# Attention on one core: row maxima run 12 steps ahead of the scores instead of 16, and the first tile's heads are divided in the attention's last step

## The chip, the cores and the metric

The kernel runs on one core of a Trainium2 chip. The metric is the device time of one execution in microseconds; the figure for a kernel is the median of several executions. A core has five engines that run side by side and wait for each other by semaphores: PE (matmul), DVE (vector), ACT (activation functions), POOL (general) and SP, which here issues all the transfers. Transfers run on 16 DMA engines.

## The reference

The program computes four residual layers on x of shape (4, 1024, 256): attention, a feed-forward layer with spikes, a selective scan, and the feed-forward layer again. Only the attention is touched.

```python
query = qt_c + qt_r            # 16 heads of 16, compact part plus rotary part
key = kt_c + kt_r
attn = jnp.einsum('bhqd,bhkd->bhqk', query, key) / scale
attn = jax.nn.softmax(attn, axis=-1)
out = jnp.einsum('bhqk,bhkd->bhqd', attn, value)
out = out.transpose(0, 2, 1, 3).reshape(b, s, d_model)
return out @ Wo_w + Wo_b
```

## The kernel before

**Stages.** `project` makes queries, keys and values of all eight tiles of 512 tokens and writes queries and keys, split in three bf16 parts each, to DRAM. `attend` works through 16 groups (4 batches x 4 groups of 4 heads). `merge_heads` divides the heads by the softmax sums, multiplies by Wo and adds to x, tile by tile. Each stage is a block: all engines leave it before the next one begins.

**A group in `attend`.** A group has 16 steps: 2 halves of the 512 queries by 8 tiles of 128 keys. In a step PE makes the scores of 4 heads in two pairs (L763), ACT takes exp of each pair (L826), and PE multiplies the probabilities of the step before by the values (`pv`, L809). Since exp needs the row maximum subtracted, three rows of the negated maxima (split in bf16 parts) stand below the queries in `qs`, and the keys have rows of ones. So all maxima of a half must be known before its first score. They come from scores made once more in the other orientation, 128 queries by 512 keys: 64 such units in a group, 4 in each step, PE's `for_max` (L749) into three banks in turn, DVE's `maximum` (L840).

**How far ahead.** In the 16 steps of group g all 64 units of group g + 1 are made, so the maxima run 16 steps ahead. Those of group 0 are made at the end of `project`: 32 pairs of units, each one reduction of 128x1024 (L499). The last group makes none.

**From maxima to rows.** When a half's 32 units are there, DVE merges the two key halves (`both_halves`, L846), PE transposes (`turn`, L756), DVE negates (L853), POOL splits in four instructions (`split`, L703 to L711), and SP sends three rows into `qs` (`max_rows`, L632). The transposition is done in step `TURN_NOW` = 2 for half 1 of this group and in step `TURN_NEXT` = 10 for half 0 of the next. PE waits for the rows of half 0 ahead of step 0 and for those of half 1 ahead of step 8 (`max_rows_in`).

**Order on the queues.** All orders are written out by hand. SP per group: rows of half 1, the 13 loads of queries and keys of group g + 2 (`load_stack`), rows of half 0 of g + 1, the stores of both halves of the output (`o_to_dram`, L636). POOL: split of half 1, values of g + 1 (`v_of`), split of half 0 of g + 1, bias addition. Loop: PE, DVE, ACT and POOL go through 5 turns of 3 groups, and the last group stands by itself after it.

**The last group** also prepares the division of batches 0 to 2 (`early_batches`): SP loads the softmax sums and the heads of tiles 0 to 2 (L540), DVE takes reciprocals and splits them (`split_recips`, L547 to L555) in step 4, SP writes the parts to DRAM (L650), waits, and reads them back in another layout (`recip_heads`, L654). `merge_heads` does the same for batch 3 and then loads the heads of tiles 3 to 7 when their buffers are free. For each tile PE spreads the reciprocals over the heads' rows (`spread_tile`, L1022), DVE multiplies (`divide`, L1068), PE projects (L1032) and DVE adds (L1075).

## Time and profile before

| | us |
|---|---|
| median of 3 runs | 2026.62 |
| lowest, highest | 2025.83, 2028.26 |
| profiled execution | 2029.69 |
| its span | 2027.7 |

Stages in the span: projection up to 183.8 (its last 38 us are the maxima of group 0), attention 184.4 to 937.3, merge 939.8 to 978.3, then feed-forward, scan and feed-forward up to the end. Busy over the span: PE 92%, DVE 80%, ACT 54%, POOL 34%; the mean granted clock of PE is 0.957 of full speed.

A line of a time line gives start, duration, engine, source line, operation, tiles (output <- input, partitions x elements, type) and how many instructions are drawn together; in brackets the idle time of the engine before it and who ended it. SPq stands for SP's transfer issues; their duration is that of issuing, not of landing.

### The profile page before, as it was taken

What the parts mean: (1) busy time and instruction counts of PE and PEld (TensorE: products, weight loads), DVE (VectorE), ACT (ScalarE), POOL (GpSimd) and SP (SyncE); (2) the same over time, 40 slices, a digit from 0 to 9 for tenths busy, and PEclk for the clock granted to TensorE, in tenths of its full rate; (3) what the DMA queues carried; (4) which work ended last, traced back from release to release, by engine and by line L of the source; (5) the groups of instructions that cost most, each with busy time, mean ns of one, the idle gap of its engine ahead of it and who ended that gap; (6) DMA issues with size and microseconds to landing.
All of it is one profiled execution on the core that took longest, in us unless ns stands there. A gap on an engine that the chain in (4) does not pass through costs nothing. (4 is left out here: it accounts for less than half of the span.)

```text
span 2027.7 us, 25794 instructions
## 1 busy us (share of the span) xinstructions
PE 1868.1 (92%) x7414; PEld 826.8 (41%) x7414; DVE 1625.9 (80%) x2596; ACT 1087.7 (54%) x1511; POOL 697.9 (34%) x474
## 2 busy tenths in 40 slices
PE   7898999999999999999999997798889877789998
PEld 4441332332322322323676663333333333356665
DVE  6878998998998988974556666999999999955654
ACT  5552665666665666674244335766576657333321
POOL 3561000001100000010000015999999999800000
PEclk9996998999998999999999997899999999899999
DMA  4850222122221122203210003455545545400000
GB/s 134 175 129 13 62 51 42 45 43 44 46 45 44 43 48 38 48 12 122 82 42 21 22 23 118 126 143 136 135 121 142 137 122 164 99 6 16 22 21 21
DMA packets 100394, 147.13 MB, mean 73 GB/s; under 512 B 15089, under 2 KB 54401, under 8 KB 98721
## 3 DMA queue, kind: packets, MB, share of 16 engines
q1 hardware_dynamic: 100256, 145.42, 28.6%
q8 instruction: 72, 1.18, 0.3%
q14 instruction: 66, 0.53, 0.1%
HBM read 114.69 MB, written 30.29 MB: 71 GB/s over the span
## 5 line engine op out<-in xcount | busy, mean ns | idle before, releaser
L840 DVE TENSOR_REDUCE mx<-max_bank 128x1 f32<-128x512 f32 x960 | 618.1, 687 | 65.0 <-PE max_bank L749 64.7
L826 ACT ACTIVATE probs<-score_bank 128x1024 f32<-128x1024 f32 x512 | 496.9, 1021 | 289.7 <-PE score_bank L763 288.8
L749 PE MATMUL max_bank<-ks,qs 96*128 96x512 bf16 x960 | 336.0, 390 | 0.0
L763 PE MATMUL score_bank<-qs,ks 99*128 99x512 bf16 x1024 | 313.6, 388 | 14.5 <-issue 10.4
L1639 PE MATMUL ys_bank<-outs,rec_diag 128*128 128x512 f32 x512 | 260.2, 642 | 67.3 <-POOL outs L1582 43.5
L1574 POOL TENSOR_TENSOR ring<-u,bc 128x1024 f32<-128x1024 f32 x128 | 300.6, 2359 | 0.4 <-DMA bc<-bc_scr 0.3
L809 PE MATMUL o_bank<-probs,vg 128*32 128x512 f32 x2048 | 275.5, 610 | 0.5 <-ACT probs L826 0.5
L1780 ACT ACTIVATE a_bank<-dt,decay_s 128x512 f32<-128x512 f32 x256 | 170.7, 686 | 150.5 <-DVE ring L1904 98.1
L1582 POOL TENSOR_TENSOR outs<-ring,bc 128x1024 f32<-128x1024 f32 x102 | 239.9, 2352 | 13.6 <-DVE ring L1904 13.6
L1252 PE MATMUL y_bank_f<-wpr_f,hid_f 128*128 128x256 f32 x1024 | 236.4, 379 | 0.0
L703 POOL CAST neg_parts<-neg_max 16x128 bf16<-16x128 f32 x31 | 8.7, 282 | 639.1 <-DVE neg_max L853 639.1
L1252 PEld LDWEIGHTS y_bank_f<-wpr_f,hid_f 128*128 128x128 f32 x1024 | 193.4, 190 | 59.9 <-issue 38.3
L1324 ACT ACTIVATE relu_f<-hid_bank_f 128x512 f32<-128x512 f32 x128 | 76.3, 596 | 250.9 <-PE hid_bank_f L1243 225.3
L749 PEld LDWEIGHTS max_bank<-ks,qs 96*128 96x128 bf16 x960 | 94.1, 98 | 281.1 <-DVE mx L840 187.1
L1895 DVE SCALAR_TENSOR_TENSOR ring<-a_bank,ring 128x512 f32<-128x512 f32 x256 | 172.6, 674 | 22.5 <-ACT a_bank L1780 21.6
L1639 PEld LDWEIGHTS ys_bank<-outs,rec_diag 128*128 128x128 f32 x512 | 99.3, 202 | 207.6 <-issue 114.9
L1414 DVE SCALAR_TENSOR_TENSOR hid_f<-hid_bank_f,relu_f 128x512 f32<-128x512 f32 x128 | 86.9, 688 | 97.0 <-ACT relu_f L1324 95.2
L763 PEld LDWEIGHTS score_bank<-qs,ks 99*128 99x128 bf16 x1024 | 99.6, 100 | 123.1 <-issue 27.4
L1904 DVE TENSOR_TENSOR_SCAN ring<-a_bank,state,ring 128x512 f32<-128x512 f32 x100 | 127.8, 1278 | 0.0
L1904 DVE TENSOR_TENSOR_SCAN ring<-a_bank,ring 128x512 f32<-128x512 f32 x104 | 126.3, 1214 | 0.0
L1243 PE MATMUL hid_bank_f<-xn_f,wfc_f 128*128 128x512 f32 x256 | 116.5, 592 | 1.1 <-PEq L972 1.1
L1613 PE MATMUL work<-xn_s,wtap_s 128*128 128x512 f32 x224 | 107.0, 616 | 7.3 <-DVE x L1876 7.3
(233 smaller groups left out, 1933.7 us busy)
## 6 DMA issues: line engine op xcount, KB each, us to landing
bc<-bc_scr SPq DMA_DIRECT2D x128, 512.0 KB, 5.0
qk_parts<-parts SPq DMA_DIRECT2D x128, 96.0 KB, 1.9
qs<-qk_parts SPq DMA_DIRECT2D x128, 64.0 KB, 4.3
o_scr<-o_sb SPq DMA_DIRECT2D x32, 256.0 KB, 2.0
ks<-qk_parts SPq DMA_DIRECT2D x16, 384.0 KB, 4.7
xn_s<-xn_scr SPq DMA_DIRECT2D x8, 515.0 KB, 6.3
x<-in_x_dram SPq DMA_DIRECT2D x8, 512.0 KB, 4.3
ks<-qk_parts SPq DMA_DIRECT2D x16, 256.0 KB, 3.5
```

The costliest lines, as they stand in the source:

```text
L749: nc.tensor.matmul(max_bank[(r + a) % MB][:], qs[r][0:SROWS, half, j, qt * P:(qt + 1) * P], ks[r][0:SROWS, j, kh * TW:(kh + 1) * TW], star ...
L763: mm = nc.tensor.matmul(score_bank[pair][:, j % 2], ks[r][0:MROWS, j, kt * P:(kt + 1) * P], qs[r][0:MROWS, qh, j, :], start=True, stop=True)
L809: mm = nc.tensor.matmul(o_bank[32 * j:32 * j + 32, :], vg[r][:, kt, j], probs[:, s % 2, j], start=(kt == 0), stop=(kt == QT - 1))
L826: nc.scalar.activation(probs[:, s % 2, 2 * pair:2 * pair + 2], score_bank[pair][:], ACT.Exp, scale=SOFTMAX_SCALE).then_inc(probs_ready, 1)
L840: nc.vector.tensor_reduce(mx[:, a // HU, a % HU:a % HU + 1], max_bank[(r + a) % MB][:], AX_X, ALU.max)\
L1252: mm = nc.tensor.matmul(y_of(b), hid[:, f, b * P:(b + 1) * P], wpr[:, f], start=(f == 0), stop=(f == FC - 1))
L1574: nc.gpsimd.tensor_tensor(ring[:, g % RING], u[t % 2][:], bc[:, g % BC, 0:1].to_broadcast([P, DC, TW]), ALU.mult).then_inc(inputs, 1)
L1582: nc.gpsimd.tensor_tensor(outs[:, g % OUTS], ring[:, g % RING], bc[:, g % BC, 1:2].to_broadcast([P, DC, TW]), ALU.mult).then_inc(weighted, 1)
L1639: mm = nc.tensor.matmul(y_bank[f][:], rec_diag[:, f * NS + n], outs[:, g % OUTS, f], start=(n == 0), stop=(n == NS - 1))
L1780: nc.scalar.activation(a_bank[g % 2][:, f], dt[:, t % 2, f], ACT.Exp, scale=a_col[:, f, n:n + 1])\
L1895: nc.vector.scalar_tensor_tensor(x, a, 1.0, x, ALU.subtract, ALU.mult).then_inc(scaled, 1)
L1904: nc.vector.tensor_tensor_scan(a if on_dve(g) else x, a, x, state[:, f, n:n + 1] if t % TPB else 0.0, ALU.mult, ALU.add)\
```

## The change

`AHEAD_STEPS` = 12 sets how far the maxima run ahead, and `STILL` = 4 follows from it.

- In the projection 24 pairs are made instead of 32. The pairs of half 1 (n from 16) keep the maxima of the two key halves apart, in `mx`, so that group 0 can finish them.
- In steps 0 to 3 of each group the last 16 units of that same group are made, in steps 4 to 15 the first 48 of the next (`maxima_of`). The last group thus makes 16 units too.
- The key halves are merged at the end of steps 3 and 11, and `TURN_NOW`, `TURN_NEXT` become 4 and 12. PE waits for the next group's queries and keys in step 4 instead of step 0.
- PE no longer waits for the first memset of the values' tile at the start.
- In the last group DVE's `split_recips` is done in step 9 instead of step 4. Ahead of the last product PE waits for the read-back reciprocals and spreads those of tile 0; DVE waits for the loaded heads and divides tile 0, ahead of its last copy (`divide_tile`). `merge_heads` starts with tile 1.
- SP's wait for the stored outputs moves from the end of `attend` into `merge_heads`, behind the load of `ident` and ahead of that of the sums. DVE's `split_recips` there comes behind the division of tile 1.

```diff
+AHEAD_STEPS = 12
+
+
 def first_groups(m):
...
         ("qs0", [P, 2, G, TW], BF16), ("qs1", [P, 2, G, TW], BF16), ("ks0", [P, G, S], BF16), ("ks1", [P, G, S], BF16),
-        ("ident", [P, P], F32), ("row_max", [P, 2, units // 2], F32), ("neg_max", [units // 2, 2, P], F32),
+        ("ident", [P, P], F32), ("mx", [P, 2, units], F32), ("row_max", [P, 2, units // 2], F32), ("neg_max", [units // 2, 2, P], F32),
         ("neg_rest", [units // 2, 2, P], F32), ("neg_parts", [units // 2, 2, 3, P], BF16), ("b_row", [P, D], F32))}
...
         PAIRS = G * QT
+        FIRST_PAIRS = 2 * AHEAD_STEPS
         max_banks = (rot_banks, comp_banks)
...
             pe.wait_ge(stack_in, 2 * STACK_LOAD)
-            for n in range(PAIRS):
+            for n in range(FIRST_PAIRS):
                 half, j, qt = n // (PAIRS // 2), n % (PAIRS // 2) // 4, n % 4
...
             nc.vector.tensor_tensor(begun["b_row"][:], bias_bank[:, 0:D], bo[:], ALU.add).then_inc(bias_kept, 1)
-            for n in range(PAIRS):
+            for n in range(FIRST_PAIRS):
                 half, i = n // (PAIRS // 2), n % (PAIRS // 2)
                 dve.wait_ge(unit_ready, n + 1)
-                nc.vector.tensor_reduce(row_max[:, half, i:i + 1], max_banks[n % 2][:].rearrange("p a t -> p (a t)"),
-                                        AX_X, ALU.max).then_inc(unit_max, 1)
+                if half == 0:
+                    nc.vector.tensor_reduce(row_max[:, 0, i:i + 1], max_banks[n % 2][:].rearrange("p a t -> p (a t)"),
+                                            AX_X, ALU.max).then_inc(unit_max, 1)
+                else:
+                    nc.vector.tensor_reduce(begun["mx"][:, 1, 2 * i:2 * i + 2], max_banks[n % 2][:], AX_X, ALU.max)\
+                        .then_inc(unit_max, 1)
                 if n == PAIRS // 2 - 1:
...
                         .then_inc(neg_ready, 1)
-            dve.wait_ge(unit_max, PAIRS)
+            dve.wait_ge(unit_max, FIRST_PAIRS)
...
-    return {n: m.sb(n, shape, dt, side="right") for n, shape, dt in (
+    early = {n: m.sb(n, shape, dt, side="right") for n, shape, dt in (
         ("recip_heads", [3 * H, B, S], BF16), ("o_in", [P, LOADED, DC, TW], F32), ("wo", [P, DC, D], F32),
-        ("head_rows", [3 * H, D], F32), ("head_parts", [3 * H, D], BF16))}
+        ("head_rows", [3 * H, D], F32), ("head_parts", [3 * H, D], BF16), ("o_sb", [P, 2, TW], F32),
+        ("o_n", [P, 2, DC, TW], F32))}
+    early["o_out"] = [m.sem(f"o_out{i}") for i in range(2)]
+    early["spread"], early["divided"] = m.sem("spread"), m.sem("divided")
+    return early
+
+
+def divide_tile(nc, dve, t, o_n, o_in, bank, spread, divided):
+
+    for c in range(DC):
+        dve.wait_ge(spread, DC * t + c + 1)
+        nc.vector.tensor_tensor(o_n[:, t % 2, c], o_in[:, t % LOADED, c], bank[c][:], ALU.mult).then_inc(divided, 1)
...
     MB = 3
-    TURN_NOW, TURN_NEXT = 2, 10
+    STILL = STEPS - AHEAD_STEPS
+    TURN_NOW, TURN_NEXT = STILL, STILL + QT
     with ExitStack() as ctx:
...
         probs = m.sb("probs", [P, 2, G, TW])
-        mx = m.sb("mx", [P, 2, HU])
+        mx = begun["mx"]
         ident, row_max, neg_max, neg_rest, neg_parts = (
             begun[n] for n in ("ident", "row_max", "neg_max", "neg_rest", "neg_parts"))
-        o_sb = m.sb("o_sb", [P, 2, TW])
+        o_sb, o_n = early["o_sb"], early["o_n"]
         EARLY = (B - 1) * H
...
         o_kept = m.sem("o_kept")
-        o_out = [m.sem(f"o_out{i}") for i in range(2)]
+        o_out, spread, divided = (early[n] for n in ("o_out", "spread", "divided"))
         sums_in, recip_split, recips_out, recips_in, early_in = (
...
-            return max_bank[(r + 1 + 4 * (s + 1)) % MB]
+            return max_bank[(r + 4 * (s + 1 + AHEAD_STEPS)) % MB]
+
+        def maxima_of(g, r, s, i):
+
+
+            if s < STILL:
+                return g, r, 4 * (s + AHEAD_STEPS) + i
+            return g + 1, (r + 1) % 3, 4 * (s - STILL) + i
...
                 body(g, g % 3, g < NGT - 1, g < NGT - 2)
-            for h in range(2):
-                sp.wait_ge(o_out[h], 16 * NGT + 16)
             sp.wait_ge(recips_in, 48)
...
             pe.sem_inc(pv_done, 3 * STEPS)
-            pe.sem_inc(max_ready, UNITS)
+            pe.sem_inc(max_ready, 4 * AHEAD_STEPS)
             pe.sem_inc(turned, 1)
...
                         pe.wait_ge(ones_set, 4)
-                    if s == 0 and with_next:
+                    if s == STILL and with_next:
                         pe.wait_ge(stack_in[(r + 1) % 3], it * STACK_LOAD + STACK_LOAD * (1 + (r + 1) // 3))
...
                         scores(g, r, s, pair)
-                        if with_next:
+                        if with_next or s < STILL:
                             if s in (TURN_NOW + 1, TURN_NEXT + 1) and pair == 0:
...
                                 pe.wait_ge(neg_ready, g * 2 + (2 if s == TURN_NOW + 1 else 3))
-                            for_max(g + 1, (r + 1) % 3, 4 * s + pair)
-                    if with_next:
-                        for_max(g + 1, (r + 1) % 3, 4 * s + 2)
+                            for_max(*maxima_of(g, r, s, pair))
+                    if with_next or s < STILL:
+                        for_max(*maxima_of(g, r, s, 2))
                     if s > 0:
...
-                            pe.wait_ge(reduced, g * UNITS + UNITS + 4 * s + 2 + MB)
+                            pe.wait_ge(reduced, g * UNITS + 4 * (s + AHEAD_STEPS) + 2 + MB)
                         turn(g if s == TURN_NOW else g + 1, 1 if s == TURN_NOW else 0, turn_bank(r, s))
-                    if with_next:
-                        for_max(g + 1, (r + 1) % 3, 4 * s + 3)
+                    if with_next or s < STILL:
+                        for_max(*maxima_of(g, r, s, 3))
+                if not with_next:
+                    pe.wait_ge(head_set, 1)
+                    pe.wait_ge(recips_in, 48)
+                    pe.wait_ge(neg_ready, g * 2 + 2)
+                    for c in range(DC):
+                        nc.tensor.matmul(max_bank[c][:], head_parts[:, c * P:(c + 1) * P], recip_heads[:, 0, 0:TW],
+                                         start=True, stop=True).then_inc(spread, 1)
                 if r == 2 or not with_next:
...
-            pe.wait_ge(ones_set, 1)
             groups(pe, body)
...
         def _(dve):
-            dve.sem_inc(reduced, MB + UNITS)
-            dve.sem_inc(row_max_ready, 2)
+            dve.sem_inc(reduced, MB + 4 * AHEAD_STEPS)
+            dve.sem_inc(row_max_ready, 1)
             dve.sem_inc(neg_ready, 1)
...
                             keep_o(g, 0)
-                        if with_next:
-                            maximum(g + 1, (r + 1) % 3, 4 * s + i)
-                        elif s == 4 and i == 0:
+                        if with_next or s < STILL:
+                            maximum(*maxima_of(g, r, s, i))
+                        elif s == QT + 1 and i == 0:
                             dve.wait_ge(sums_in, 16)
                             split_recips(nc, dve, sums, recip_parts, recip_split)
-                    if s == QT - 1 and with_next:
+                    if s == STILL - 1:
+                        both_halves(g, 1)
+                    if s == STILL + QT - 1 and with_next:
                         both_halves(g + 1, 0)
-                if with_next:
-                    both_halves(g + 1, 1)
+                if not with_next:
+                    dve.wait_ge(early_in, 16 * DC * LOADED)
+                    divide_tile(nc, dve, 0, o_n, o_in, max_bank, spread, divided)
                 if r == 2 or not with_next:
...
         PT = 8
-        recip_heads, o_in, wo, head_parts = (early[n] for n in ("recip_heads", "o_in", "wo", "head_parts"))
+        recip_heads, o_in, wo, head_parts, o_n, o_out, spread, divided = (
+            early[n] for n in ("recip_heads", "o_in", "wo", "head_parts", "o_n", "o_out", "spread", "divided"))
         sums = m.sb("sums", [H * PT, S // PT])
         recip_parts = m.sb("recip_parts", [H * PT, 3, S // PT], BF16)
-        o_n = m.sb("o_n", [P, 2, DC, TW])
         spread_bank = [m.bank(f"spread_bank{c}") for c in range(DC)]
...
         heads_in = [m.sem(f"heads_in{i}") for i in range(LOADED)]
-        spread, divided, out_ready, x_new = (m.sem(n) for n in ("spread", "divided", "out_ready", "mh_x_new"))
+        out_ready, x_new = m.sem("out_ready"), m.sem("mh_x_new")
         by_rows = o_scr.rearrange("g (j r) t -> (g j) r t", r=2 * HD)
...
+            sp.dma_start(ident[:], io["ident"]).then_inc(ident_in, 16)
+            for h in range(2):
+                sp.wait_ge(o_out[h], 16 * B * NG + 16)
             sp.dma_start(sums[:], by_rows[HEADS0:, HD, :].rearrange("g (h t) -> g h t", h=PT)).then_inc(sums_in, 16)
-            sp.dma_start(ident[:], io["ident"]).then_inc(ident_in, 16)
             sp.wait_ge(recip_split, 5)
...
-            spread_tile(0)
             for t in range(NT):
...
                     dve.wait_ge(out_ready, DC * (t - 1))
-                for c in range(DC):
-                    dve.wait_ge(spread, DC * t + c + 1)
-                    nc.vector.tensor_tensor(o_n[:, t % 2, c], o_in[:, t % LOADED, c], spread_bank[c][:], ALU.mult)\
-                        .then_inc(divided, 1)
+                divide_tile(nc, dve, t, o_n, o_in, spread_bank, spread, divided)
...
-            divide(0)
-            dve.wait_ge(sums_in, 16)
-            split_recips(nc, dve, sums, recip_parts, recip_split)
             for t in range(NT):
...
                     divide(t + 1)
+                if t == 0:
+                    dve.wait_ge(sums_in, 16)
+                    split_recips(nc, dve, sums, recip_parts, recip_split)
                 if t == 3:
...
```

## Rows read from the trace of the kernel before

**Rows 1.** Table of stretches, core 0, 193 to 238.5 us: busy us of each engine, clock, DMA.
```profile
193.00:238.50 45.50, 45.50 (x262) 13.80 (x258) 42.12 (x69) 30.82 (x32) 4.58 (x10) 1.00 0.22 48
```

**Rows 2.** Time line of DVE, the projection's tail: start us, us, what.
```profile
173.20 1.22 DVE L499 TENSOR_REDUCE row_max<-comp_banks 128x1 f32<-128x1024 f32 x1
...
182.61 1.22 DVE L499 TENSOR_REDUCE row_max<-comp_banks 128x1 f32<-128x1024 f32 x1
```

**Rows 3.** Time line of SP's queue, the same tail.
```profile
171.50 1.86 SPq L239 DMA_DIRECT2D qs<-neg_parts  x3
```

**Rows 4.** DMA issues, 165 to 176 us: issue xcount, KB each, us to landing.
```profile
qs<-neg_parts SPq DMA_DIRECT2D x3, 4.0 KB, 1.7
```

**Rows 5.** Time line, the first group's start: POOL and PE.
```profile
184.41 0.53 POOL L686 MEMSET vg<- 128x512 f32 x1 [12.93 <-POOLq L139]
...
185.46 1.03 PE L763 MATMUL score_bank<-qs,ks 99*128 99x512 bf16 x2 [2.90 <-POOL vg L686]
```

**Rows 6.** Time line of PE, first group: the first scores of two steps.
```profile
199.03 0.60 PE L763 MATMUL score_bank<-qs,ks 99*128 99x512 bf16 x2
...
201.86 0.60 PE L763 MATMUL score_bank<-qs,ks 99*128 99x512 bf16 x2
```

**Rows 7.** Time line of PE: transpositions either side of one turn of the loop.
```profile
310.34 0.28 PE L756 MATMUL max_bank<-ident,row_max 128*16 128x128 f32 x1
...
340.62 0.28 PE L756 MATMUL max_bank<-ident,row_max 128*16 128x128 f32 x1
```

**Rows 8.** Time line of the last group, all engines.
```profile
900.90 0.19 DVE L846 TENSOR_REDUCE row_max<-mx 128x16 f32<-128x32 f32 x1
901.07 1.04 PE L763 MATMUL score_bank<-qs,ks 99*128 99x512 bf16 x4
...
905.30 1.04 PE L763 MATMUL score_bank<-qs,ks 99*128 99x512 bf16 x4
...
909.53 1.14 PE L763 MATMUL score_bank<-qs,ks 99*128 99x512 bf16 x4
...
909.80 1.77 SPq L632 DMA_DIRECT2D qs<-neg_parts  x3
...
920.19 0.69 DVE L859 COPY o_sb<-o_bank 128x512 f32<-128x512 f32 x1
...
920.27 0.34 SPq L650 DMA_DIRECT2D recip_scr<-early_parts  x1
...
935.44 1.06 PE L809 MATMUL o_bank<-probs,vg 128*32 128x512 f32 x8 [0.47 <-ACT probs L826]
...
936.57 0.69 DVE L859 COPY o_sb<-o_bank 128x512 f32<-128x512 f32 x1 [15.69 <-PE o_bank L809]
```

**Rows 9.** DMA issues, 900 to 950 us: issue xcount, KB each, us to landing.
```profile
recip_scr<-early_parts SPq DMA_DIRECT2D x1, 288.0 KB, 6.6
recip_heads<-recip_scr SPq DMA_DIRECT2D x3, 96.0 KB, 2.9
```

**Rows 10.** Time line of the merge, all engines.
```profile
939.78 0.59 SPq L995 DMA_DIRECT2D sums<-o_scr  x1
...
942.74 5.43 PE L1032 MATMUL out_bank<-wo,o_n 128*128 128x256 f32 x16
...
947.34 1.26 SPq L540 DMA_DIRECT2D o_in<-o_scr  x2
...
952.29 0.60 PE L1022 MATMUL spread_bank<-recip_heads,head_parts 48*128 48x512 bf16 x2
...
953.74 1.29 DVE L1068 TENSOR_TENSOR o_n<-o_in,spread_bank 128x512 f32<-128x512 f32 x2 [0.65 <-DMA o_in<-o_scr]
...
956.48 0.60 PE L1022 MATMUL spread_bank<-recip_heads,head_parts 48*128 48x512 bf16 x2
```

**Rows 11.** Table of stretches, core 0: an idle of PE and what followed.
```profile
1652.40:1656.10 3.70, 0.00 (x0) 0.00 (x0) 3.70 (x6) 1.85 (x4) 3.70 (x3) 1.00 0.46 123
1656.10:1659.50 3.40, 3.35 (x4) 1.14 (x4) 3.40 (x5) 0.14 (x1) 3.40 (x2) 0.52 0.32 108
```

## The prediction

> **What bounds the kernel now.** The profiled execution took 2029.69 us, its span 2027.7; the median of the three runs is 2026.62. I work out a difference in the profiled execution and take it from all three, since the change adds no work that depends on the run. The change touches four stretches, so I read each with the view that shows its pace.
>
> First the table of stretches: in the loop over groups PE is busy in all of its 45.50 us at full clock, DVE in 42.12 and ACT in 30.82 [rows 1]. A step with maxima is 201.86 - 199.03 = 2.83 us long, PE-bound [rows 6]. Second the time line of the projection's tail: one reduction of a pair follows the other on DVE without a gap; nothing else is left to do there [rows 2]. Third the last group, which makes no maxima: its steps 2 and 3 take 909.53 - 905.30 = 4.23 us, 2.115 each, set by ACT, for whose exponentials PE waits, and steps 0 to 3 together 909.53 - 901.07 = 8.46 [rows 8]. Last, the start of the merge: a wait for stored outputs, a new block, a chain of small transfers, and only then a steady PE [rows 10].
>
> **Part 1, eight pairs leave the projection.** Pair 24 (counted from 1) starts at 173.20, pair 32 at 182.61: eight pairs are 9.41 us, all of it on DVE and on the path [rows 2]. The reduction of 128x1024 into two columns instead of one reads the same elements; I cost that at nothing, and at most 8 x 0.05 us if the second output column mattered. What is late next is the other thing that the projection's end waits for: the three rows of negated maxima of half 0. SP issues them from 171.50 for 1.86 us [rows 3], each lands 1.7 us after its issue [rows 4]; the last was issued about 172.7, so it lands at 174.4. DVE's new last reduction ends at 173.20 + 1.22 = 174.42. They tie. I take **-9.3**, between -9.4 and -8.7 (the landing is read from a median).
>
> **Part 2, PE no longer waits for the first memset.** Its first score came at 185.46 with POOL's memset named, while POOL itself began at 184.41 and needed 0.53 [rows 5]. PE could have started at most about 1.0 earlier, and at least 0 if its own entry takes as long. I take **-0.5**. The value tile is still waited for, a step and a half later.
>
> **Part 3, sixteen units move into the last group.** Counts per group are otherwise equal: 64 units in every one, now 16 of this group and 48 of the next. Steps 0 to 3 of the last group go from 8.46 to 4 x 2.835 = 11.34 us: **+2.9**. PE's time in which it waited for ACT is already subtracted in this. The range is 2.7 to 3.2, for DVE's copy of the other half's output falls among the four steps.
>
> **Part 4, the rows of maxima have four steps, not six.** From the start of the step that transposes, the chain transposition, negation, four POOL instructions and three SP issues was 909.80 + 1.77 - 905.30 = 6.3 us [rows 8]; the last of three issues begins 0.6 before the end of 1.77, and with 1.7 to land [rows 4] it is 7.4. In a group with maxima it has 4 x 2.84 = 11.3 us; in the last group 4 x 2.115 = 8.46. Both cover it, the second by 1.1 only. SP's 13 stack loads follow the rows of half 1 in the queue as before and end well before the rows of half 0, eight steps later, as before. POOL's copies of values and the bias additions keep their places behind the splits. Scores of the next half are queued behind such a wait on PE, and ACT and DVE behind them; cost **0**, at most 0.5 in the last group. The merging of both key halves (0.19 us on DVE [rows 8]) now comes one step ahead of the transposition; DVE has (45.50 - 42.12) / 16 = 0.21 us idle per step to take it [rows 1], so 0, between -0.1 and +0.1 for each of 31.
>
> **Part 5, the early denominators come later, and the last step waits for them.** Let T be the start of step 4 of the last group. Before, everything counted from step 2 (905.30). SP's rows go out at T + 4.5 to T + 6.3, then the sums, then six loads of heads, as before [rows 8]. DVE's five instructions now start behind its copy of the first half: that ran at 920.19, 10.66 after step 4, for 0.69. So they run from T + 11.4 to T + 17.1 (before, they ended at 920.24). The write of the parts was issued at 920.27 and landed 6.6 us later, at 926.9, which is 21.6 after 905.30, because the loads of heads and weights stood before it; the readback took 0.85 to its last issue and 2.9 to land [rows 9]. The loads drain at the same T + 21 now. If the write lands with them, at T + 21.6, the readback lands at T + 25.4. PE is through with the product of step 14 at 935.44 - 0.47 = 934.97 = T + 25.4. So the new wait is almost exactly covered. Behind it stand the two spreading matmuls (0.60 us [rows 10]) and the last product, which before started at 935.44 (T + 25.9) after ACT [rows 8]; it starts at T + 26.1 to 26.5. DVE divides for 1.29 before its last copy [rows 10], which starts at about T + 27.5 where it started at 936.57 = T + 27.0 [rows 8]: **+0.5**. Bounds: +0.2 when the readback is early, +2.3 when the write takes its whole 6.6 us from T + 17.1.
>
> The write of 288 KB shows 6.6 us behind the loads [rows 9]. The Trainium skill, "DMA: Bandwidth & Descriptors", section "Queues, rings and completion order", says that each DMA engine takes descriptors in ring order; by it the new, later write still leaves with the loads and ends at T + 21.6, where a transfer that overtook them would end at about T + 20. The first gives the +0.5, the second +0.35.
>
> **Part 6, the merge.** Let K be the end of the last copy, 937.26 before. The next block began at 939.78 = K + 2.5, behind the landing of the stored outputs; without that wait it begins at about K + 0.7, for the block of the attention began at 184.41, 0.58 after DVE's last reduction had ended at 183.83 [rows 2, 5]. Tile 0 is divided already, so its projection can start at K + 1.5 instead of K + 5.5. That would be 4 us, but the load of tile 3 stands in the way. It is issued behind sums, split, write and readback of the last batch: 947.34, and DVE already waited 0.65 us for it, until 953.74 = K + 16.5 [rows 10]. That chain starts from the landing of the stored outputs, which doesn't move; it wins only the block's entry, of which I take 0.4 us (the whole was 0.58). So DVE has tile 3 divided at K + 16.1 + 1.3 = K + 17.4, and PE, which before started spreading tile 4 at 956.48 = K + 19.2, starts then: -1.8. From there PE's pace holds, 956.48 - 952.29 = 4.19 us per tile [rows 10]. But PE would have ended tile 2 at about K + 13.6: it stands idle for 3.8 us where it was busy. An idle of 3.70 us at full clock was followed by 3.40 us at 0.52, that is the 1.2 GHz level [rows 11]. Half of 3.4 is 1.7 us lost. The sum is **-0.1**, between -1.8 (the clock holds, or PE is slow from the block's start and so has no idle) and +1.7 (the low level lasts 7 us).
>
> **Sum:** -9.3 - 0.5 + 2.9 + 0 + 0.5 - 0.1 = -6.5 us. Span 2021.2, profiled execution 2023.2, median **2020.1**.
>
> One thing varies by itself: where the loop turns over (after every third group) PE stops and the clock falls. Eight steps are 22.7 us; across the first such point it was 340.62 - 310.34 = 30.28, 7.6 more [rows 7]. There are four of them; I allow 3 us either way for all.
>
> **The rivals.**
> (a) The clock holds in the merge, part 6 gives -1.8: 2018.4. For it: PE is low from the start if the block's entry idles it long enough. Against it: [rows 11]. Chance 0.2.
> (b) Tile 3's load isn't the gate, since it lands sooner in an emptier queue; the merge then gives 4.0 and, if the clock holds too, 1.8 of its first projection (5.43 where a later one has 4.19 - 0.60): -12.2, 2014.4. Against it: DVE already waited for it. 0.08.
> (c) The readback is late (+2.3, not +0.5) and the clock low for long in the merge (+1.7, not -0.1): -2.9, 2023.7. 0.13.
> (d) Slower: the rows of maxima are late in every half of a group. Place: PE's wait ahead of the first score of a half. The price is what the chain lasts beyond four steps, about 31 times; it decides from 11.3 us, where the chain shows 7.4. Another POOL or SP item ahead of it worth 4.7 us would make 0.8 x 31 = 25, less the 6.5: 2045. Such an item, the stack loads, stands behind it in the queue. 0.04.
> (e) The change doesn't do what it says: the projection's end isn't DVE's but a transfer's, so eight pairs free nothing; 2029.4. [rows 2] to [rows 4] speak against it. 0.02.
>
> **How the numbers follow.** The forecast has 0.53, with its own range of 2017.5 to 2022.5. Its parts' bounds, the clock at the loop's turns and cases (a) and (c) give 2014.5 to 2024.5; left out are (d), (e), and (b), which lies at the lower end. What a measurement here can tell from no change is 0.2%, 4.05 us. Within it lie (c), (e) and 0.03 of the forecast's: 0.18. Slower is (d), 0.04, and faster the rest, 0.78.
>
> **What would show it.** The projection's last reduction at 174.4 and POOL's memset 9.3 earlier than 184.41; PE's first score about 0.5 behind it or less. Steps of 2.84 through step 3 of the last group. No idle of PE ahead of scores of a half. In the last step PE idle under 0.5 us for the readback. In the merge a PE idle of 3 to 4 us ahead of the spreading of tile 4, ended by DVE, which waited for the load, and a granted clock of 0.5 behind it. Wrong would be: rows of maxima that PE waits for, an idle over 1 us ahead of the last product, or PE steady from the first tile.

## The result, and the profile after

| | before | after |
|---|---|---|
| median, us | 2027.44 (4 executions) | 2016.18 (4 executions) |
| lowest to highest | 2025.83 to 2028.5 | 2011.42 to 2018.74 |
| profiled execution / its span | 2029.69 / 2027.7 | 2018.74 / 2016.9 |
| ratio | | 0.9936, 95% interval 0.9924 to 0.9948 |

The change is faster, by 11.3 us between the medians (13 by the ratio) where -6.5 was forecast. With the executions of the later studies, in which both kernels were run again unchanged, the means are 2028.1 (113 executions, standard error 0.25) and 2017.24 (17, standard error 0.9): **-10.9 us**, 95% interval about -12.7 to -9.1. That is the number to be explained.

The page of the changed kernel, its head and first row: PE is as busy as before (92%).

```profile
span 2016.9 us, 25815 instructions
PE 1862.0 (92%) x7414; PEld 828.5 (41%) x7414; DVE 1627.6 (81%) x2605; ACT 1087.4 (54%) x1511; POOL 697.9 (35%) x474
```

The time line of the changed kernel where projection turns into attention, as [rows 2, 3, 5] for before:

```profile
169.61 1.86 SPq L243 DMA_DIRECT2D qs<-neg_parts  x3
...
171.31 1.22 DVE L507 TENSOR_REDUCE mx<-comp_banks 128x2 f32<-128x1024 f32 x1
173.14 0.53 POOL L711 MEMSET vg<- 128x512 f32 x1 [3.55 <-POOLq L142]
...
174.08 1.03 PE L788 MATMUL score_bank<-qs,ks 99*128 99x512 bf16 x2 [2.82 <-SPq L647]
```

The first pair began at 144.04 in this execution and at 145.94 in that of before, so starts are compared as distances from it. The last reduction ends at 172.53, 28.49 behind the first pair: pair 24 of before ended at 28.48. A reduction of 1.22 us is as long as it was. PE's first score comes 1.55 us behind the last reduction; before, it came 1.63 behind.

The last group on PE, as [rows 8]:

```profile
884.54 1.06 PE L841 MATMUL o_bank<-probs,vg 128*32 128x512 f32 x8
885.54 0.60 PE L788 MATMUL score_bank<-qs,ks 99*128 99x512 bf16 x2
...
889.32 1.07 PE L841 MATMUL o_bank<-probs,vg 128*32 128x512 f32 x8
890.32 0.39 PE L774 MATMUL max_bank<-ks,qs 96*128 96x512 bf16 x1
890.54 0.60 PE L788 MATMUL score_bank<-qs,ks 99*128 99x512 bf16 x2
...
896.21 1.03 PE L788 MATMUL score_bank<-qs,ks 99*128 99x512 bf16 x4
897.17 1.06 PE L841 MATMUL o_bank<-probs,vg 128*32 128x512 f32 x8
898.17 0.28 PE L781 MATMUL max_bank<-ident,row_max 128*16 128x128 f32 x1
```

Steps 0 to 3 run from 885.54 to 896.21: 10.67 us. Steps 2 and 3 last 2.84 each (890.54 to 896.21); 0 and 1 together 5.00, since the product that belongs to step 0 was already done ahead of it (884.54) and only one follows until 890.54. With T = 896.21, the rest of that group on SP, DVE and PE:

```profile
900.70 1.77 SPq L659 DMA_DIRECT2D qs<-neg_parts  x3
...
913.20 0.34 SPq L677 DMA_DIRECT2D recip_scr<-early_parts  x1
917.87 1.26 SPq L681 DMA_DIRECT2D recip_heads<-recip_scr  x3
```

```profile
907.48 3.34 DVE L566 RECIPROCAL early_sums<-early_sums 96x512 f32<-96x512 f32 x1
...
912.49 0.69 DVE L574 TENSOR_TENSOR early_parts<-early_sums,early_parts 96x512 bf16<-96x512 f32 x1
922.38 1.29 DVE L552 TENSOR_TENSOR o_n<-o_in,max_bank 128x512 f32<-128x512 f32 x2 [9.20 <-PE max_bank L826]
923.58 0.68 DVE L890 COPY o_sb<-o_bank 128x512 f32<-128x512 f32 x1
```

```profile
921.90 0.59 PE L826 MATMUL max_bank<-recip_heads,head_parts 48*128 48x512 bf16 x2 [0.25 <-issue]
922.42 1.06 PE L841 MATMUL o_bank<-probs,vg 128*32 128x512 f32 x8
```

The rows of maxima go out at T + 4.49, the readback at T + 21.66, the spreading is at T + 25.69 with an idle of 0.25 before it, the last copy begins at T + 27.37. With K = 924.26, the end of that copy, the merge shows on PE and in the table of stretches (us, PE busy, granted clock, DMA share, GB/s):

```profile
925.23 0.59 PE L1058 MATMUL spread_bank<-recip_heads,head_parts 48*128 48x512 bf16 x2 [1.75 <-PEq L591]
925.75 3.72 PE L1068 MATMUL out_bank<-wo,o_n 128*128 128x256 f32 x16
...
934.12 3.72 PE L1068 MATMUL out_bank<-wo,o_n 128*128 128x256 f32 x16
940.83 1.03 PE L1058 MATMUL spread_bank<-recip_heads,head_parts 48*128 48x512 bf16 x2 [2.99 <-DVE o_n L552]
941.79 6.58 PE L1068 MATMUL out_bank<-wo,o_n 128*128 128x256 f32 x16
```

```profile
937.84:940.83 2.99, 0.00 (x1) 0.99 0.48 145
940.83:944.30 3.47, 3.47 (x8) 0.50 0.54 201
944.30:960.00 15.70, 15.70 (x62) 0.89 0.67 208
```

PE idles 2.99 us ahead of the spreading for tile 4 and is then granted half its clock, for the 3.47 us of the second row and longer: a mean of 0.89 over the 15.7 us of the third row is about 3.4 us more, so 6.8 us in all. The spreading takes 1.03 us instead of 0.60 and the sixteen matmuls behind it 6.58 instead of 3.72, together 3.3 us lost. On DVE it is the load of tile 3 that ends the wait:

```profile
939.49 1.28 DVE L552 TENSOR_TENSOR o_n<-o_in,spread_bank 128x512 f32<-128x512 f32 x2 [5.10 <-DMA o_in<-o_scr]
```

**Stretch by stretch.** Each number is a mean of five profiles. Before: the kernel before three times and two with one wait moved or left out, which changed nothing (before_again, before_third, before_late_wait, before_no_memset_wait, all below). After: the changed kernel four times and one with a wait moved, which changed nothing either (after_again, after_third, after_fourth, after_wait0).

| stretch | before | after | difference | forecast |
|---|---|---|---|---|
| first pair of maxima to first score | 39.50 | 30.06 | -9.44 | -9.8 |
| first score to first transposition | 10.47 | 15.47 | +5.00 | |
| first to last transposition, without the loop's turns | 594.67 | 595.23 | +0.56 | |
| last transposition to last product | 28.18 | 24.02 | -4.16 | |
| last product to end of last copy (K) | 1.82 | 1.85 | +0.03 | |
| these four together | 635.14 | 636.57 | +1.43 | +3.4 |
| four turns of the loop, 8 steps each | 115.64 | 113.98 | -1.66 | 0 |
| K to the feed-forward's first matmul | 41.67 | 41.49 | -0.18 | -0.1 |
| sum | | | -9.85 | -6.5 |

The rows for the transposition move by two steps with it (from step 2 to step 4), so only their sum means something. Ahead of the first pair and behind the merge nothing is changed: the first pair begins anywhere from 141.7 to 146.6 us in these ten profiles, and the stretch behind the merge scatters by 5 us, in kernels of either kind. The merge's own difference has a standard error of 0.4 us, that of the first group 0.4, that of the turns 1.2.

### The profile page after: what moved, and what is told of

Same layout as the page of the kernel before. It is cut to its first block and busy times, and to the rows that moved or that the text cites. A ratio compares the mean times of both kernels' runs of the same rounds, so it can differ in the third digit from the quotient of the medians.

```text
span 2016.9 us, 25815 instructions
## 1 busy us (share of the span) xinstructions
PE 1862.0 (92%) x7414; PEld 828.5 (41%) x7414; DVE 1627.6 (81%) x2605; ACT 1087.4 (54%) x1511; POOL 697.9 (35%) x474
## 5 line engine op out<-in xcount | busy, mean ns | idle before, releaser
L871 DVE TENSOR_REDUCE mx<-max_bank 128x1 f32<-128x512 f32 x976 | 628.1, 687 | 62.4 <-PE max_bank L774 61.3
L1927 DVE SCALAR_TENSOR_TENSOR ring<-a_bank,ring 128x512 f32<-128x512 f32 x256 | 171.5, 670 | 22.5 <-ACT a_bank L1812 21.6
```

What stands on the lines that cost most here:

```text
L871: nc.vector.tensor_reduce(mx[:, a // HU, a % HU:a % HU + 1], max_bank[(r + a) % MB][:], AX_X, ALU.max)\
L1927: nc.vector.scalar_tensor_tensor(x, a, 1.0, x, ALU.subtract, ALU.mult).then_inc(scaled, 1)
```

## The experiments

### Which part of the change brings it

Four kernels ran together: both kernels again, and each half of the change by itself. maxima_only is the changed kernel with tile 0 divided in `merge_heads`, as before (SP's wait for the stored outputs and DVE's `split_recips` of the last batch go back to their old places with it):

```diff
-                if not with_next:
-                    dve.wait_ge(early_in, 16 * DC * LOADED)
-                    divide_tile(nc, dve, 0, o_n, o_in, max_bank, spread, divided)
...
+            spread_tile(0)
...
+            divide(0)
```

merge_only is the changed kernel with the maxima 16 steps ahead, all reductions and PE's wait for the memset as before, and the split of the early denominators in step 4, as before:

```diff
-AHEAD_STEPS = 12
+AHEAD_STEPS = 16
...
-    TURN_NOW, TURN_NEXT = STILL, STILL + QT
+    TURN_NOW, TURN_NEXT = 2, 10
...
-                elif s == QT + 1 and i == 0:
+                elif s == 4 and i == 0:
```

> The kernel before, unchanged, for a second profile. Theory 1 (the part of the gain that the forecast lacks is the chance of PE's clock, at the four turns of the loop and ahead of the projection's tail): ratio 1.000, but the transpositions either side of the four turns, 116.8 us in all in the first profile, are 2 us or more off that here, and so is the first reduction of a pair, at 145.9 in the first. Theory 2 (the change itself shortens these stretches): both within 1 us of the first profile.

> The changed kernel, unchanged, for a second profile and a surer ratio. The first profile has 113.3 us across the four turns and the first pair at 144.0. Theory 1: these scatter here by 2 us or more as well, and the ratio lies nearer to the 0.9955 that the local differences of the stages touched make (-9.5 tail, -0.5 first group, +2.2 and +0.3 last group, +0.6 merge: -6.9, plus the start of the first group). Theory 2: 113.3 and 144.0 come again, within 1 us, and the ratio is 0.994 or lower.

> Only the maxima: 12 steps ahead, 24 pairs in the projection, no wait for the first memset, early reciprocals in step 9. Tile 0 is divided in the merge as before. Theory 1: -9.5 - 0.5 + 2.2 = -7.8 us, ratio 0.996. Theory 2 with the hidden gain on this side: -11 to -13 us, ratio 0.994.

> Only the merge: maxima 16 steps ahead as before, early reciprocals in step 4, but tile 0 divided in the last step, and SP's wait for the stored outputs in the merge. Theory 1: the last copy 0.3 us later and the merge 0.6 longer for its idle and low clock, +0.9 us, ratio 1.0005. Theory 2 with the hidden gain on this side: -3 us or more, ratio 0.9985 or lower.

| kernel | median, us | ratio to before |
|---|---|---|
| before_again | 2027.55 (12 executions) | 1.0003 (0.9990 to 1.0016) |
| after_again | 2018.05 (6) | 0.9940 (0.9921 to 0.9960) |
| maxima_only | 2014.49 (6) | 0.9938 (0.9915 to 0.9962) |
| merge_only | 2028.28 (12) | 1.0000 (0.9990 to 1.0010) |

The whole effect is that of the maxima. Dividing tile 0 early is worth nothing (parts 5 and 6 together, forecast +0.4). In merge_only the spreading in the last step falls into the time in which PE waited for ACT and costs nothing: the last product starts 28.18 us behind the last transposition, as before, the last copy ends level, and the merge behind it took 42.85 us.

The expectations set two theories against each other, chance at the turns and a gain that the change brings. The two profiles did not decide: after_again's turns took 116.6 us where the first profile had 113.3, and its first pair began at 146.6 instead of 144.0, as chance would have it; its ratio stayed at 0.9940, as the other theory would.

### The turns of the loop

Across the first turn before took 7.6 us more than eight steps inside the loop [rows 7]. The table of stretches (PE alone) of before at this turn, the pause and what follows:

```profile
324.69:328.60 3.91, 1.39 (x13) 0.98 0.19 73
328.60:338.23 9.63, 9.63 (x26) 0.50 0.02 4
338.23:340.62 2.39, 2.39 (x14) 0.91 0.00 0
```

The same in maxima_only, whose first turn stayed at full clock after a pause as long:

```profile
314.14:316.55 2.41, 0.00 (x1) 1.00 0.27 103
316.55:326.20 9.65, 9.65 (x51) 1.00 0.02 7
```

In 9.6 us the first got through 26 matmuls and the second 51. I first thought of the one wait that stands in step 0 in the kernel before and in step 4 in the changed one, that of PE for the next group's queries and keys. Two kernels move it alone: after_wait0 (the changed kernel, the wait back in step 0) and before_late_wait (the kernel before, the wait behind the first pair of scores).

```diff
-                    if s == STILL and with_next:
+                    if s == 0 and with_next:
```

```diff
                     for pair in range(2):
                         scores(g, r, s, pair)
+                        if s == 0 and with_next and pair == 0:
+                            pe.wait_ge(stack_in[(r + 1) % 3], it * STACK_LOAD + STACK_LOAD * (1 + (r + 1) // 3))
```

Two more, before_flat and after_flat, write the loop over groups of either kernel out straight on all engines, so that there are no turns:

```diff
-            with eng.Fori(0, (NGT - 1) // 3) as it:
+            for it in range((NGT - 1) // 3):
```

> The kernel before with the attention's loop over 15 groups written out straight, on all engines, so that nothing turns over. Three profiles of kernels with 16 steps ahead have 116.0 us across the four turns where 4 x 22.9 = 91.6 would be the pace inside; so -24 us, ratio 0.988. If the pause at a turn is the fetch of instructions and comes in straight code too, nothing.

> The changed kernel, written out straight in the same way. Theory A (what the forecast lacks lies in the turns: the changed kernel loses less to PE's low clock behind them): it differs from before_flat by the sum of the local differences alone, -9.5 tail - 0.2 first group - 0.2 pace + 2.5 last group + 0.4 merge = -7.0 us, so -31 against the kernel before, ratio 0.985. Theory B (the missing gain lies elsewhere): it stays 11 to 12 us under before_flat, ratio 0.982 or 0.983.

> The changed kernel with one piece undone: PE waits for the next group's queries and keys in step 0, as before, not in step 4. Theory A1 (this wait with its register arithmetic stands ahead of the first score behind each turn and lengthens PE's pause): pause 2.66 us on average instead of 2.54, low clock 7.6 us instead of 5.1 per turn, 4 us longer than the changed kernel, ratio 0.996. Theory A2 (chance, or another piece): as the changed kernel, 0.994.

> The kernel before with that same wait behind the first pair of scores of step 0 instead of ahead of it. Theory A1: the pause at a turn is 0.1 us shorter and the low clock behind it rarer, -4 us, ratio 0.998. Theory A2: 1.000.

| kernel | median, us | ratio to before |
|---|---|---|
| before_flat | 2008.28 (5) | 0.9895 (0.9879 to 0.9910) |
| after_flat | 1999.81 (4) | 0.9866 (0.9849 to 0.9882) |
| after_wait0 | 2017.05 (7) | 0.9951 (0.9934 to 0.9968) |
| before_late_wait | 2027.71 (12) | 0.9998 (0.9990 to 1.0007) |

The wait is not it: put back, it leaves the changed kernel where it was, and put later, it leaves before where it was. Written straight, the kernel before is 20 us faster, where 24 were expected. The four turn stretches alone fall by 22.8 us (115.6 to 92.9) and the other groups by 2.1, but in the seven straight profiles the first pair of maxima begins 3.8 us later than in the 13 with a loop (147.9 and 144.1 in the mean); why is not shown. In before_flat the same place (PE alone) has no pause and full clock throughout:

```profile
324.00:345.00 21.00, 20.96 (x119) 1.00 0.20 52
```

Without turns the change brings 7.1 us between the means of executions (2007.33 and 2000.27, standard error of the difference 1.5), where it brings 10.9 with them (standard error 0.9). The stretches without turns and merge give -8.4 in the straight kernels (the mean of after_flat, flat_load3 and flat_best against the one profile of before_flat).

### How far ahead, and the bounds of parts 1, 4 and 6

These were tried on the straight kernel, which scatters less. flat_ahead14 and flat_ahead11 are after_flat with `AHEAD_STEPS` = 14 (28 pairs in the projection) and 11 (22 pairs); flat_maxima_only is maxima_only written straight. flat_load3 is after_flat with the heads of tile 3 loaded ahead of the wait for the stored outputs:

```diff
             sp.dma_start(ident[:], io["ident"]).then_inc(ident_in, 16)
+            sp.wait_ge(divided, DC)
+            load_heads(sp, by_rows, o_in, LOADED, heads_in[0])
             for h in range(2):
                 sp.wait_ge(o_out[h], 16 * B * NG + 16)
...
-            for t in range(LOADED, NT):
+            for t in range(LOADED + 1, NT):
```

> The changed kernel written out straight, and in the merge SP loads the heads of tile 3 ahead of its wait for the stored outputs. If that load was the gate (part 6 of the prediction), PE's idle of 3 us ahead of spreading tile 4 and the low clock behind it (16 matmuls in 6.58 us instead of 3.72) go: -6 us against after_flat, 1994, ratio 0.983 or 0.984. If not (rival b), nothing: 2000.

> The changed kernel written out straight, maxima 14 steps ahead: 28 pairs in the projection, two steps with maxima in the last group. By the terms of parts 1 and 3: four pairs more, +4.7, two long steps fewer, -1.2: +3.5 us against after_flat. If the gain were due to the last group or to another place of the transpositions, it would be 8.5 us slower, like before_flat.

> The same with 11 steps ahead: 22 pairs, five steps with maxima in the last group, transpositions in steps 5 and 13. Terms: -2.35 + 0.6 = -1.7, but by part 4 the rows of maxima (7.4 us from the step's start) no longer fit in three short steps of the last group (6.3): +1.1 there, and in the other groups 8.5 us just cover 7.4 to 8.4. Sum -0.6 us against after_flat. If the rows are late in every group (rival d), PE waits at 30 places: +10 us or more.

> Only the maxima, written out straight: the merge as before. The difference to after_flat is the worth of the merge part without the turns' scatter. Forecast of it +0.4 us lost (the last copy 0.3 later, the merge 0.1 better); measured in single profiles 0.3 + 0.6 = 0.9 lost. So this kernel should be 0.5 to 1 us faster than after_flat; if the division in the last step gains what it saves at the start of the merge, 3 to 4 us slower.

| kernel | pairs in the projection | median, us | first pair to first score |
|---|---|---|---|
| before_flat | 32 | 2008.28 (5) | 39.30 |
| flat_ahead14 | 28 | 2004.74 (4) | 34.48 |
| after_flat | 24 | 1999.81 (4) | 29.83 |
| flat_ahead11 | 22 | 2003.47 (4) | 29.82 |
| flat_maxima_only | 24 | 2000.40 (4) | 29.82 |
| flat_load3 | 24 | 1998.86 (5) | 29.82 |

With 22 pairs the last reduction ends 2.4 us earlier and the first score comes at the same distance; the forecast was 0.6 us faster than after_flat, and it is 3.7 slower. The time line of flat_ahead11 there:

```profile
171.60 1.20 DVE L507 TENSOR_REDUCE mx<-comp_banks 128x2 f32<-128x1024 f32 x1
171.80 0.42 POOL L283 TENSOR_TENSOR neg_parts<-neg_rest,neg_parts 16x128 bf16<-16x128 f32 x1
172.24 1.84 SPq L243 DMA_DIRECT2D qs<-neg_parts  x3
175.75 0.53 POOL L711 MEMSET vg<- 128x512 f32 x1 [3.53 <-POOLq L142]
...
176.49 1.01 PE L788 MATMUL score_bank<-qs,ks 99*128 99x512 bf16 x2 [5.05 <-SPq L647]
```

DVE is done at 172.80. The last of the three rows is issued about 0.6 us before the end of SP's issuing, at 173.5, and lands 1.7 us later, at 175.2 (the same 1.7 us as in [rows 4]); SP waits for that landing at the end of `project`. The new block's first instruction comes at 175.75, 0.57 behind it, as it came 0.58 behind DVE's last reduction in the kernel before. In the changed kernel the last row landed at 172.6 by the same reckoning, DVE's work ended at 172.53 and POOL began at 173.14. So at 24 pairs both ends meet, and below it the landing of the rows is the floor. In the last group the rows of half 1 now have three short steps to arrive, and PE waits for them (PE of flat_ahead11):

```profile
884.79 1.06 PE L841 MATMUL o_bank<-probs,vg 128*32 128x512 f32 x8
886.94 1.04 PE L788 MATMUL score_bank<-qs,ks 99*128 99x512 bf16 x4 [1.09 <-DMA qs<-neg_parts]
```

1.09 us here, where the chain of the prediction gives 7.4 - 3 x 2.115 = 1.06. Two halves in the groups of 2.84 us a step waited as well, 0.65 us at 613.1 and 0.38 at 636.5, so there the chain took up to 3 x 2.84 + 0.65 = 9.2 us, and the groups as a whole took 1.4 us longer than in after_flat. In the changed kernel the only idles of over 0.3 us ahead of a score in the groups are the four turns of the loop. flat_load3 and flat_maxima_only don't differ from after_flat. flat_load3 was expected to gain 6 us, the idle of 2.99 and the low clock behind it; but in after_flat's own profile that idle was only 1.46 us and no low clock followed it, so there was little to gain. The load brings tile 3 earlier, and the idle moves to the tile before (1.32 us), since the sums behind the load came later and DVE stood 5.17 us for them.

### Half way in the loop, part 2 alone, and the best version

loop_ahead14 is the changed kernel, with its loop, and `AHEAD_STEPS` = 14; before_no_memset_wait is the kernel before without PE's `wait_ge(ones_set, 1)` at the start of `attend`; after_third is the changed kernel once more. flat_best is after_flat with the heads of tiles 3 and 4 loaded ahead of the wait for stored outputs, as in flat_load3, and the last denominators split later:

```diff
-                if t == 0:
+                if t == 2:
                     dve.wait_ge(sums_in, 16)
                     split_recips(nc, dve, sums, recip_parts, recip_split)
```

> The changed kernel with its loop, 14 steps ahead: transpositions in steps 2 and 10, as in the kernel before. Local terms: tail -5.0, attention +0.0, merge -0.4: -5.4. If the turns cost less with any kernel of the changed form, another -4: -9.4, ratio 0.9955, and 112 us across the turns. If the place of the transpositions behind a turn is what matters: -5.4, ratio 0.9973, and 116.

> The kernel before without PE's wait for the first memset (part 2 alone): by the forecast -0.5 us (0 to -1.0), ratio 0.9998. The first score against the last reduction tells it in the profile: 1.63 us behind it before, 1.55 in the changed kernel, so -0.1 is what the traces so far give. If the start's shift is what changes the turns: 112 across them and -4 us.

> The changed kernel once more, for four more turns. With chance alone the twelve turns of its three profiles come nearer to the 29.0 us of the kernel before (low clock 7.7 us each); with a cause in the change they stay near 28.0 (5.1).

> Written out straight, 12 steps ahead; in the merge SP loads the heads of tiles 3 and 4 ahead of its wait for the stored outputs, and DVE makes the last batch's reciprocals behind the division of tile 3, not of tile 1. flat_load3 showed the gate move: the sums landed 3 us later behind the loads, and DVE's divisions stood behind them (PE idle 1.3 us). If that is the whole of it, PE runs steady from tile 1 and this takes 1.5 to 3 us off flat_load3: 1996 to 1997, ratio 0.984. If the last batch's reciprocals then come too late for tile 6, PE waits there and nothing is gained.

| kernel | median, us | ratio to before |
|---|---|---|
| loop_ahead14 | 2021.93 (12) | 0.9968 (0.9957 to 0.9979) |
| before_no_memset_wait | 2028.92 (12) | 1.0008 (0.9994 to 1.0022) |
| after_third | 2015.37 (3) | 0.9938 (0.9917 to 0.9959) |
| flat_best | 1999.63 (5) | 0.9865 (0.9844 to 0.9886) |

Part 2 alone is nothing: from the first pair to the first score it is 39.53 us, against 39.50. loop_ahead14 has -4.81 at the projection's end and +0.6 in its groups and last group without turns, so -4.2, and gained 6.5; its turns took 110.3 us, and one of the four stayed at full clock. Its transpositions stand in steps 2 and 10, as in the kernel before, so on this one profile their place is not what makes turns cheap. Its merge was 2.6 us shorter than the mean of before. PE lost its clock at the start of the block, and behind the idle ahead of tile 4 it kept it:

```profile
926.61 5.41 PE L1068 MATMUL out_bank<-wo,o_n 128*128 128x256 f32 x16
...
941.97 0.60 PE L1058 MATMUL spread_bank<-recip_heads,head_parts 48*128 48x512 bf16 x2 [1.58 <-DVE o_n L552]
942.50 3.72 PE L1068 MATMUL out_bank<-wo,o_n 128*128 128x256 f32 x16
```

flat_best, meant to beat after_flat by 3 us, didn't. PE no longer idles ahead of tile 4 but does so two tiles later (PE and DVE of flat_best):

```profile
931.05 0.59 PE L1061 MATMUL spread_bank<-recip_heads,head_parts 48*128 48x512 bf16 x2 [2.02 <-DVE o_n L552]
931.57 5.41 PE L1071 MATMUL out_bank<-wo,o_n 128*128 128x256 f32 x16
```

```profile
929.62 1.28 DVE L552 TENSOR_TENSOR o_n<-o_in,spread_bank 128x512 f32<-128x512 f32 x2 [4.02 <-DMA o_in<-o_scr]
```

The gate was moved, not removed: the load of tile 5 is the one behind the chain now, and the low clock follows it (5.41 us for sixteen matmuls that take 3.72).

### More turns

before_third and after_fourth are the kernel before and the changed one, once more, for their turns.

> The kernel before, unchanged, once more, for its four turns of the loop. So far five profiles of kernels that run 16 steps ahead show 113.8 to 116.8 us across the four turns (mean 115.6), and no turn of their 20 without low clock behind it. Theory (the turns are dearer with 16 steps ahead): 115 to 117 again and none of four without low clock. Rival (chance, both kinds have the same mean of about 114): as likely below 114 as above. Time 2027 to 2029.

> The changed kernel, unchanged, once more, for its four turns. Five profiles of kernels that run 12 steps ahead show 105.9 to 116.6 us across the turns (mean 111.9), and 5 turns of 20 without low clock. Theory: 110 to 113, and about one turn of four without low clock. Rival (chance): 114 or more is as likely as less. Time by the first 2015 to 2017, ratio 0.994; by the rival, with the local parts of -8.1 us alone, 0.996.

before_third took 2027.98 us (10 executions, ratio 1.0001, 0.9992 to 1.0011), its turns 114.9; after_fourth 2020.22 (4, 0.9954, 0.9938 to 0.9971), its turns 116.4, and none of its four stayed at full clock. The first lies at the edge of what the theory said (115 to 117, none at full clock), the second doesn't come out as it said (110 to 113). All profiles with a loop together:

| kernels | four turns, us in each profile | mean | low clock behind a turn, mean | turns without it |
|---|---|---|---|---|
| 16 steps ahead, 6 profiles | 116.8, 116.4, 114.8, 116.3, 113.8, 114.9 | 115.5 | 7.1 us | 0 of 24 |
| 12 steps ahead, 6 profiles | 113.3, 116.6, 105.9, 112.5, 111.1, 116.4 | 112.6 | 5.4 us | 5 of 24 |

Order: before, before_again, merge_only, before_late_wait, before_no_memset_wait, before_third; after, after_again, maxima_only, after_wait0, after_third, after_fourth. The difference of 2.9 us has a standard error of 1.7; dealt out at random, two sets of six differ by as much in 11 of 100 cases. The turns alone don't settle it. What speaks for it from outside is the whole time: executions differ by 10.9 us (0.9) where the stretches without turns give 9.44 - 1.43 + 0.18 = 8.2, a surplus of 2.7, with a standard error of about 1.1 once those of the first group and the merge are added. Without a loop there is none (7.1, standard error 1.5, against 8.4). In loop_ahead14 the surplus is 6.5 - 4.2 = 2.3 with its merge left out; with the 2.6 us of its merge nothing is left of it, so it decides nothing.

One record speaks against it. The mean granted clock is known for 109 executions of the kernel before (0.9552) and 17 of the changed one (0.9569). As time at half clock, twice the span times the missing share, that is an estimated 181.7 and 173.6 us: 8.1 less, with a standard error of 2.9 (8.5 less with maxima_only and after_wait0 counted in). The projection's tail, which is at half clock throughout in the profiles, is 9.4 us shorter by itself. So over all executions no fall of the low clock is left for the turns, where the six profiles of either kind show 4 x (7.1 - 5.4) = 6.8 us.

## Why the prediction was right or wrong

The direction and the place of the gain were right, the size was not: -6.5 where about -10.9 is so. The median of 2016.18 lies outside the forecast's own 2017.5 to 2022.5 and inside the wide range. Of the 4.4 us that are missing, the stretches without turns account for 1.7: parts 3 and 5 and the first group were too dear, part 2 erred the other way. The rest, 2.7 us, the sum had put at zero: the turns of the loop are the likely place, and it is not shown.

**Part 1: right.** -9.3 forecast; part 1 and 2 together -9.44. The last reduction ended where the row of pair 24 said, two output columns cost nothing, and the tie with the rows of half 0 is real: flat_ahead11 shows the floor at once. The floor is the landing, as the prediction had it.

**Part 2: wrong by 0.5.** I read the releaser named (POOL's memset) as the bound. PE's first score came 1.55 behind the last reduction instead of 1.63, and before_no_memset_wait shows that the wait cost nothing: PE's own way into the block takes as long. The bound 0 was named, the value taken was not it.

**Part 3: mis-sized by 0.7.** I counted four steps at 2.84; they took 10.67, not 11.34, so +2.2 and not +2.9. The missing 0.67 is in step 0, whose product stands ahead of it. Where ACT sets the pace (before) this made no difference, where PE does (now), it does. The first group too took 0.7 less than two more steps would (+5.00 for 5.68): it starts at low clock, and its length varies by 2 us among kernels that are alike there, so this is scatter.

**Part 4: right.** No idle of PE ahead of a half's scores; the chain's 7.4 us are confirmed in the last group by the 1.09 us of flat_ahead11. In the other groups it took up to 9.2 us there, more than I read and still under the 11.3 that it has. Inside the loop 25 intervals took 572.6 us where they had taken 572.8.

**Part 5: mechanism right, 0.4 too dear.** The write landed with the loads, T + 21.6 forecast, the readback issued at T + 21.66; 4.6 us from issue to landing (913.20 to 917.8) where the 6.6 of [rows 9] would have made 919.8. The Trainium skill says that a DMA engine takes descriptors in ring order ("DMA: Bandwidth & Descriptors", section "Queues, rings and completion order"), and the trace agrees: the last load ahead of the write, that of the weights, was issued at 908.72 and took 8.6 us, until 917.3, and the write landed 0.5 behind it; before, they landed at 926.4 and 926.9. The spreading came at T + 25.69 (forecast T + 25.4 at the earliest) and the last copy at T + 27.37 against T + 27.04 before. In the other four profiles the last product was 0.3 earlier, so the mean cost is 0.1.

**Part 6: the order of events right, two sizes off that cancel.** Forecast: block entry at K + 0.7, first projection at K + 1.5, wait for tile 3 until K + 16.1, idle of 3.8, then 3.4 us of low clock, sum -0.1. The rows: K + 0.93, K + 1.49, K + 15.23, 2.99, and low clock for 6.8. The spreading for tile 4 came at K + 16.57, 2.6 us earlier than before where 1.8 were forecast, and the low clock cost 3.3 us where 1.7 were. Together that is +0.65 in this execution (42.05 against 41.40), so the forecast's -0.1 owes something to luck. I took the length of the low clock from one place [rows 11]; the same kernel's merge stood at half clock twice as long, from 939.8 to 946.2. The mean over five profiles is -0.18 (standard error 0.4), and merge_only and the pair after_flat and flat_maxima_only find no effect.

**What the sum lacked, as far as is known: the turns.** The prediction set the four turns to zero, as a thing that "varies by itself", 3 us either way. The profiles have -1.7 (five of either kind, standard error 1.2) to -2.9 us (six, 1.7) there, and the executions a surplus of 2.7 over all other stretches. That is the largest error, and this is the step that failed: a stretch that costs 24 us (115.5 against 4 x 22.9) was taken as noise with the same mean in both kernels, though the change moves what runs in the steps behind the pause. That the surplus is at the turns is supported (it is gone where there are no turns) but not shown: the turns' own numbers differ as much by chance in 11 of 100 cases, and the granted clock over all executions shows no fall beyond the projection's tail. Where the 2.7 us arise, and why a turn at times keeps its clock, stays open. PE's instructions just ahead of the pause are the same, the pause is as long (2.3 to 2.9 us in both), and the one wait that differs there is ruled out.

Together: the start gave 0.4 us less than forecast, the groups cost 2.0 less and the merge 0.1 less, which makes -8.2; with 1.7 to 2.9 at the turns it is -9.9 to -11.1. The rest to the first comparison's 11.3 to 13 is its four executions, whose mean of 2015.6 lies 1.6 below the mean of all 17.

**The rivals.** (a) has PE at low clock from the start of the merge and a gain of 1.8 there. In the five profiles of the changed form the clock fell behind the idle each time (in after_third at the block's start as well). In loop_ahead14 and after_flat it came as (a) says: 5.41 us for the first sixteen matmuls, full clock behind an idle of 1.58 and 1.46, and a merge of 39.0 and 38.9 us, 2.6 and 2.8 less than the mean of before. So the merge varies by execution between this course and that of the forecast. (b) is out, since PE did wait for tile 3's load; of (c), the low clock was as long as it says in the profiled execution (6.8 us), but the readback wasn't late; (d) would have shown idles ahead of each half, there are none; (e) is excluded by the table of pairs. The time landed near (b)'s, for none of (b)'s reasons.

**The best version.** after_flat and the three kernels built on it at 24 pairs take 1999.7 us in the mean of 18 executions, 28.4 less than before and 17.5 less than the changed kernel. Nothing behind the straight loop (loads moved, tile 0 divided early or not) differs from it by more than the scatter.

## What to carry to other kernels

Work moved out of a stretch with nothing beside it (8 reductions, 9.4 us) into one with cover costs what it adds to the bound engine there: read the two paces, and look at the step at either end separately. When the loop's edges show a pause with a fall of the clock, price the edge first: here straight code was worth 20 us, more than the whole change. And a term that "varies by itself" needs several profiles of both kernels before it may be put to zero.

## What the runs showed of the hardware that was not expected

- A turn of the loop over groups costs PE 2.3 to 2.9 us of pause and then 0, 3.4, 6.8 or 10.2 us at half clock: 2.8 to 7.6 us over the pace, 5 to 6 in the mean. The same pause is at times followed by no fall at all (314.14 to 326.20 in maxima_only). Straight code has neither.
- Idles of PE in the merge: those of 1.32 us (flat_load3), 1.46 (after_flat) and 1.58 (loop_ahead14) were not followed by low clock, those of 2.02 (flat_best) and 2.99 (the changed kernel) were. In the first four PE had been at low clock at the start of the block. The merge of loop_ahead14 was the shortest of all with a loop (39.03 us).
- A block's first instruction came 0.58 and 0.61 us behind DVE's last reduction in the kernel before and the changed one, and 0.57 behind the landing of the last row of maxima in flat_ahead11, where DVE had been done for 2.95 us.
